# Attention with relative positions on one core: a narrower band product, moved behind the weighted sum, with its ends filled by GpSimd, and row maxima turned once a step

## The chip, the cores and the metric

The kernel runs on one core of a Trainium2 chip. The metric is the time of one execution on the device in microseconds (us). Its parts are TensorE (matmuls, PE, with its weight loads PEld), ScalarE (ACT), VectorE (DVE), GpSimd (POOL), SyncE (SP, which issues DMAs), the working memory SBUF and the matmul outputs' memory PSUM.

## What is computed

The reference is one transformer block: attention with 16 heads of 16 features on 8 sequences of 1024 tokens, a layer norm, a feed-forward layer with binarized weights and a second layer norm. The part that matters here is the attention with its relative bias:

```python
scores = jnp.einsum('bhid,bhjd->bhij', qh, kh)
rel = jnp.clip(pos[None, :] - pos[:, None], -K, K) + K
bias_r = jnp.einsum('bhid,rd->bhir', qh, rel_pe)
bias = jnp.take_along_axis(bias_r, jnp.broadcast_to(rel[None, None], (b, h, l, l)), axis=-1)
attn = jax.nn.softmax(scores + bias, axis=-1)
out = jnp.einsum('bhij,bhjd->bhid', attn, vh)
```

K is 64, so that a query has 129 different biases. Beyond a distance of 64 tokens the bias is that of an end of the table, and the kernel adds it to the keys beforehand. Only a band around the diagonal is left: for 128 queries, some 256 keys.

## The kernel before

Three stages follow each other: the projections (to about 250 us), the attention, and from about 2050 us the output projection with the feed-forward layer. The change touches the attention alone (lines 539 to 1138).

The attention goes over 64 steps, one for two heads of a sequence. The heads' rows lie in the upper and the lower half of the TensorE array, and their matmuls run side by side. Every engine has its own program for a step, and the order in each is written out by hand. A step on TensorE has eight pairs m of two units (pair, L1111), and it works on three things at once:

- Weighing, for this step's heads. A unit is one tile of 128 keys against half of the queries (512). turn_bands (L1041) transposes the parts of the band that lie in it into PSUM; only units near the diagonal have any. In pairs 0 and 4 each unit has two (over both heads), in the other pairs one unit has four and the other none, and the order of units (weighed, L638) puts the one with four first. weigh (L1059) adds the scores. ScalarE takes the exponential (expo, L899) into SBUF.
- The weighted sum of an earlier pair's exponentials with the values (weighted, L1077; lagging, L1091), eight matmul instructions.
- Looking, 24 units ahead: the scores are computed the other way round (look, L1022), and VectorE takes the maximum of each row with the band added (L933 to L963). GpSimd negates the maxima and splits them in a rounded part and a rest (minus_maxima, L807), TensorE transposes them (turn_max, L1033), ScalarE copies them out of PSUM (copy_turned, L894), and SyncE moves them into two extra rows of the queries (load_minus_max, L723), so that the scores come out of weigh with the maximum subtracted. This is done in two halves, at units 4 and 10 of a step (TURN_AT, L619).

The band product (band_product, L1008) for heads nearly three steps ahead multiplies 128 queries with the differences of the bias table. The table has 3 x 128 columns for each head: 128 differences, then 128 copies of the last one, then those for the last tile. The product has 256 columns. Every tile but the last uses the first two blocks, so that its columns 128 to 255 are all the same. ScalarE copies both heads' product to SBUF (copy_band, L886). For two tiles at a time SyncE writes them to memory (write_bands, L715), and GpSimd reads them back with rows one element shorter, which shifts each row against the one before and makes the band (read_bands, L784). GpSimd's own queue issues the loads of queries, keys and values too (step_of, L823).

Scores and band products use two PSUM buffers (weigh_ps) in turn. The order of use is first unit, band product, second unit, and then the same again with the buffers exchanged. So the band product waits for the exponential of the unit before the pair's first, the second unit for that of the first, and the next pair's first unit for the copy of the band (wait_for, L987). ScalarE's order is exponential, (in pair 1 the copy of the finished sums, L884), band copy, exponential. Each pair's order on TensorE is this:

```python
products(i, step, m, 0)
if bands_at(step, m):
    band_product(i, band_index(step, m))
lagging(i, step, m)
if step >= 0:
    turn_bands(i, step, m, 1)
products(i, step, m, 1)
```

## Time and profile before

| | |
|---|---|
| time, median of 3 runs | 2427.24 us (2426.69 to 2430.31) |
| the profiled execution, its own time | 2427.77 us |
| its span | 2426.1 us |
| TensorE busy | 2266.8 us (93%) |
| VectorE busy | 1742.5 us (72%) |
| ScalarE busy | 1669.9 us (69%) |
| GpSimd busy | 964.5 us (40%) |
| ScalarE, exponentials (L903) | 1048.8 us, 1024 of them |
| ScalarE, band copies (L891) | 302.8 us, 512 of them |
| TensorE, band products (L1017) | 202.4 us, 1024 of them |

Busy times overlap. A TensorE row's start is recorded and its end is modelled, and matmuls that are side by side or follow each other in the pipeline overlap in their durations. So the distance between two starts tells what work costs, and a row's duration tells when its result can be read. In a row of the timeline, x8 is the number of like instructions that it merges, and the brackets at its end give the idle time of the engine before it and who ended that.

### The profile page before, as it was taken

Reading aid. Unit: us, or ns where it says so; the run is one execution under the profiler, and the core shown is the slowest. Engines: PE = TensorE matmul, PEld = TensorE weight load, DVE = VectorE, ACT = ScalarE, POOL = GpSimd, SP = SyncE. Lnnn points to the kernel's source line nnn. Section 1 sums busy time; section 2 is a strip of 40 time slices with the busy share of each in tenths; the row PEclk is TensorE's granted clock in tenths of the full one; section 3 lists DMA queues with packets and bytes.
Section 4 is the critical chain, followed back from the end, with each engine's and each line's share of the span. In section 5 each row is a group of like instructions: output and inputs, shape, how many; then the busy total and the mean of one; then the engine's idle time right before and its main releaser. Section 6 shows DMA issues by size and latency. Waiting matters only on the chain. (4 is left out here: it accounts for less than half of the span.)

```text
span 2426.1 us, 47764 instructions
## 1 busy us (share of the span) xinstructions
PE 2266.8 (93%) x14642; PEld 1273.6 (52%) x14642; DVE 1742.5 (72%) x3444; ACT 1669.9 (69%) x2239; POOL 964.5 (40%) x1565
## 2 busy tenths in 40 slices
PE   4998599999999999999999999999999999799997
PEld 3555244444444444444444444444444444688886
DVE  2444467777777777777777777777777773588885
ACT  2443167777777777777777777777777777466766
POOL 0000444443444434443344433444334432466663
PEclk8999589999999999999999999999999999899999
DMA  6998777777777777777777777767767762333321
GB/s 179 357 335 317 216 186 204 204 209 207 204 207 200 208 207 204 203 205 205 204 204 204 209 207 202 204 201 208 210 199 207 201 196 88 104 99 108 108 63 44
DMA packets 335292, 468.58 MB, mean 193 GB/s; under 512 B 90517, under 2 KB 263270, under 8 KB 335206
## 3 DMA queue, kind: packets, MB, share of 16 engines
q0 software_dynamic: 120960, 215.78, 34.9%
q1 hardware_dynamic: 201206, 243.05, 30.1%
q10 hardware_dynamic: 13040, 8.80, 1.2%
q8 instruction: 30, 0.49, 0.1%
q14 instruction: 56, 0.46, 0.1%
HBM read 244.73 MB, written 221.25 MB: 192 GB/s over the span
## 5 line engine op out<-in xcount | busy, mean ns | idle before, releaser
L903 ACT ACTIVATE probs<-weigh_ps 128x1024 f32<-128x1024 f32 x1024 | 1048.8, 1025 | 403.7 <-PE weigh_ps L1069 400.4
L955 DVE CUSTOM_DVE_ANT_1 ring_ps<-ring_ps,band_all 128x512 f32<-128x512 f32 x1008 | 681.0, 715 | 265.9 <-PE ring_ps L1029 265.7
L1029 PE MATMUL ring_ps<-keys,queries 48*128 48x512 f32 x2048 | 839.2, 474 | 32.2 <-DVE partial_max L944 10.4
L1069 PE MATMUL weigh_ps<-queries,keys 50*128 50x512 f32 (+3 forms) x2688 | 752.7, 386 | 1.4 <-ACT probs L903 1.1
L944 DVE TENSOR_REDUCE partial_max<-ring_ps 128x2 f32<-128x1024 f32 x512 | 627.7, 1226 | 155.3 <-PE ring_ps L1029 115.0
L1029 PEld LDWEIGHTS ring_ps<-keys,queries 48*128 48x128 f32 x2048 | 370.6, 187 | 511.1 <-issue 394.5
L1086 PE MATMUL sum_ps<-probs,values 128*32 128x512 f32 x4096 | 547.3, 606 | 0.1
L1054 PE MATMUL weigh_ps<-ident,band_all 128*128 128x128 f32 x2048 | 362.7, 290 | 23.2 <-ACT carried L891 20.3
L1069 PEld LDWEIGHTS weigh_ps<-queries,keys 50*128 50x128 f32 x2688 | 356.7, 186 | 17.7 <-ACT probs L903 9.5
L790 POOL DMA_DIRECT2D band_all<-band_scr x320 | 230.6, 723 | 331.4 <-DMA band_scr<-carried 319.6
L1054 PEld LDWEIGHTS weigh_ps<-ident,band_all 128*128 128x128 f32 x2048 | 214.0, 141 | 246.2 <-ACT probs L903 104.6
L891 ACT ACTIVATE carried<-weigh_ps 128x512 f32<-128x512 f32 x512 | 302.8, 592 | 50.3 <-PE weigh_ps L1017 50.3
L1017 PE MATMUL weigh_ps<-rel_terms,queries 48*128 48x256 f32 x1024 | 202.4, 343 | 17.9 <-DMA queries<-q_scr 17.0
L1308 DVE TENSOR_TENSOR hidden<-gelu,hidden 128x512 fp32r<-128x512 f32 x128 | 146.3, 1160 | 46.3 <-ACT hidden L1409 45.2
L803 POOL DMA_DIRECT2D band_all<-band_scr x128 | 101.9, 796 | 187.7 <-DMA band_scr<-carried 165.2
L1478 PE MATMUL hid_ps<-x1T,sign1T 128*128 128x512 f32 x512 | 144.2, 404 | 12.9 <-ACT hidden L1409 11.6
L1407 ACT ACTIVATE gelu<-hid_ps,b_col,alpha 128x512 f32<-128x512 f32 x128 | 99.7, 779 | 77.4 <-PE hid_ps L1478 51.4
L1492 PE MATMUL out_ps<-sign2T,hidden 128*128 128x256 f32 x1024 | 150.4, 290 | 0.6 <-ACT hidden L1409 0.6
L955 DVE DVE_READ_ACCUMULATOR2_ANT partial_max<- 128x1 f32 x1024 | 145.1, 142 | 0.0
L1492 PEld LDWEIGHTS out_ps<-sign2T,hidden 128*128 128x128 f32 x1024 | 137.9, 188 | 9.5 <-ACT hidden L1409 0.8
L693 POOL DMA_DIRECT2D queries<-q_scr x128 | 80.6, 630 | 153.7 <-PE weigh_ps L1069 142.2
L1017 PEld LDWEIGHTS weigh_ps<-rel_terms,queries 48*128 48x128 f32 x1024 | 103.3, 189 | 55.1 <-ACT probs L903 30.9
(115 smaller groups left out, 1861.3 us busy)
## 6 DMA issues: line engine op xcount, KB each, us to landing
band_scr<-carried SPq DMA_DIRECT2D x256, 512.0 KB, 4.1
band_all<-band_scr POOLq DMA_DIRECT2D x128, 512.0 KB, 6.6
band_all<-band_scr POOLq DMA_DIRECT2D x128, 256.0 KB, 3.3
keys<-k_scr POOLq DMA_DIRECT2D x128, 240.0 KB, 9.0
k_scr<-k_parts SPq DMA_DIRECT2D x16, 1792.0 KB, 8.2
q_scr<-q_parts SPq DMA_DIRECT2D x16, 1024.0 KB, 6.2
queries<-q_scr POOLq DMA_DIRECT2D x128, 128.0 KB, 2.9
o_scr<-weighted_s SPq DMA_DIRECT2D x64, 256.0 KB, 9.1
```

What stands on the lines that cost most here:

```text
L790: pool.dma_start(band[:, c % SLOTS, m, :, e, c0:c1], flat(band_scr, band_base(c, m) + e * P * BAND_ROW + offset, [[BAND_ROW - 1, P], [2 * ...
L891: nc.scalar.activation(band_out[:, chunk % BANDS_OUT, :, e], weigh_ps[weigh_of["band", n]][:, :, 0:2 * P], ACT.Copy).then_inc(s_be, 1)
L903: nc.scalar.activation(probs[:, u % PROBS], weigh_ps[weigh_of["scores", at]][:], ACT.Exp).then_inc(s_pr, 1)
L944: nc.vector.reduce_max(partial_max[:, g, :, e, 0], ring_ps[:, first:second + 1], AX_X).then_inc(s_seen, HG)
L955: nc.vector.tensor_tensor_reduce(out=both, in0=both, in1=bias, scale=1.0, scalar=LOWEST, op0=ALU.add, op1=ALU.max, accum_out=partial_max[: ...
L1017: last = nc.tensor.matmul(dst[:, h, 0:2 * P].rearrange("p (a c) -> p a c", a=2), query_rows(c, h, ROWS, tile * P, (tile + 1) * P), moving, ...
L1029: nc.tensor.matmul(dst, query_rows(c, h, ROWS, tile * P, (tile + 1) * P), key_rows(c, h, ROWS, c0, c0 + 512), start=True, stop=True, tile_ ...
L1054: nc.tensor.matmul(weigh_ps[weigh_of["scores", at]][:, h, e * P:(e + 1) * P], band[:, c % SLOTS, tile // 2, h, tile % 2, side * P:(side + ...
L1069: last = nc.tensor.matmul(weigh_ps[weigh_of["scores", at]][:, h, e0 * P:e1 * P], key_rows(c, h, QROWS, k0, k0 + P), query_rows(c, h, QROWS ...
L1086: last = nc.tensor.matmul(sum_ps[r0:r0 + 32, :], values[:, c % SLOTS, v0:v0 + 32], probs[:, (2 * n + g) % PROBS, h], start=(n == 0), stop= ...
L1308: nc.vector.tensor_tensor(hidden[:, it % 2, 1, j], gelu[:, j % 2], hidden[:, it % 2, 0, j].bitcast(F32), ALU.subtract).then_inc(s_lo, 1)
L1492: last = nc.tensor.matmul(out_ps[:, t], hidden[:, it % 2, c, j, t * P:(t + 1) * P], sign2T[:, j], start=(c == 0 and j == 0), stop=(c == 1 ...
```

## The change

The band product of every tile but the last has 130 columns (NARROW), and ScalarE copies 130. GpSimd fills columns 130 to 255 from column 128 (fill_ends), for one or two tiles at a time, and SyncE's write waits for that. In TensorE's order the band product stands behind the weighted sum and the second unit's transposes, in front of the second unit's products; the order in which the PSUM buffers are used, and ScalarE's order, stay. The row maxima of both halves are negated, split, transposed, copied and moved together, at unit 10. Semaphores follow their new counts. The diff, cut to its core:

```diff
@@ -575,11 +576,11 @@
-row_max = sb("row_max", [P, 2, HG, QT], F32)
-negative = sb("negative", [P, 2, HG, QT], F32)
-negative_parts = sb("negative_parts", [P, 2, HG, PARTS, QT], F32)
-zero = sb("zero", [P, HG, QT], F32)
-minus_max = sb("minus_max", [HG * PARTS * QT, 2, P], F32R)
+row_max = sb("row_max", [P, HG, 2, QT], F32)
+negative = sb("negative", [P, HG, 2, QT], F32)
+negative_parts = sb("negative_parts", [P, HG, PARTS, 2, QT], F32)
+zero = sb("zero", [P, HG, 2, QT], F32)
+minus_max = sb("minus_max", [HG * PARTS * NT, P], F32R)
@@ -616,10 +618,10 @@
-TURN_AT = {4: 0, 10: 1}
+TURN_AT = 10
...
-    return u in TURN_AT and 0 <= step + 1 < G
+    return u == TURN_AT and 0 <= step + 1 < G
@@ -715,20 +717,20 @@
         c, m = n // NM, n % NM
-        sp.wait_ge(s_be, cnt(i, NT, 2 * n + 2))
+        sp.wait_ge(s_bf, cnt(i, NM, n + 1))
         sp.dma_start(flat(band_scr, band_base(c, m), [[BAND_ROW, P], [P * BAND_ROW, HG * 2], [1, 2 * P]]),
...
-    def load_minus_max(i, step, g):
+    def load_minus_max(i, step):
         c = step + 1
-        sp.wait_ge(s_tc, cnt(i, 2, 2 * c + g + 1))
+        sp.wait_ge(s_tc, cnt(i, 1, c + 1))
         for h in range(HG):
             r0 = h * ROW_TILE + ROWS
-            rows = queries[r0:r0 + PARTS, c % SLOTS, g * 512:(g + 1) * 512].bitcast(F32)
-            sp.dma_start(rows.rearrange("r (a p) -> r a p", a=QT),
-                         minus_max[h * PARTS * QT:(h + 1) * PARTS * QT, g, :].bitcast(F32)
-                         .rearrange("r (a p) -> r a p", a=1)).then_inc(s_min[g][c % SLOTS], 16)
+            rows = queries[r0:r0 + PARTS, c % SLOTS, :].bitcast(F32)
+            sp.dma_start(rows.rearrange("r (a p) -> r a p", a=NT),
+                         minus_max[h * PARTS * NT:(h + 1) * PARTS * NT, :].bitcast(F32)
+                         .rearrange("r (a p) -> r a p", a=1)).then_inc(s_min[c % SLOTS], 16)
@@ -804,16 +806,29 @@
-    def minus_maxima(i, step, g):
+    def minus_maxima(i, step):
         c = step + 1
-        done = cnt(i, 2, 2 * c + g + 1)
-        pool.wait_ge(s_rm, done)
-        nc.gpsimd.tensor_tensor(negative[:, g], zero[:], row_max[:, g], ALU.subtract)
-        nc.gpsimd.tensor_tensor(negative_parts[:, g, :, 0].bitcast(F32R), zero[:], row_max[:, g],
+        pool.wait_ge(s_rm, cnt(i, 2, 2 * c + 2))
+        nc.gpsimd.tensor_tensor(negative[:], zero[:], row_max[:], ALU.subtract)
+        nc.gpsimd.tensor_tensor(negative_parts[:, :, 0].bitcast(F32R), zero[:], row_max[:],
                                 ALU.subtract).then_inc(s_neg, 1)
-        pool.wait_ge(s_neg, done)
-        nc.gpsimd.tensor_tensor(negative_parts[:, g, :, 1], negative[:, g], negative_parts[:, g, :, 0],
+        pool.wait_ge(s_neg, cnt(i, 1, c + 1))
+        nc.gpsimd.tensor_tensor(negative_parts[:, :, 1], negative[:], negative_parts[:, :, 0],
                                 ALU.subtract).then_inc(s_mm, 1)
+
+    def fill_ends(i, step, quarter):
+        n = (step + BAND_STEPS) * NM + quarter - 2
+        if 0 <= n < G * NM:
+            pool.wait_ge(s_be, cnt(i, NT, 2 * n + 2))
+            pool.sem_inc(s_passed, 1)
+            tiles = 1 if n % NM == NM - 1 else 2
+            out = band_out[:, n % BANDS_OUT, :, 0:tiles]
+            last = None
+            for e in range(tiles):
+                end = out[:, :, e, P]
+                last = nc.gpsimd.tensor_copy(out[:, :, e, NARROW:2 * P],
+                                             flat(end, 0, [end.ap[0], end.ap[1], [0, P - 2]]))
+            last.then_inc(s_bf, 1)
@@ -825,23 +840,25 @@
             load_queries(pool, i, step + 3)
-        if 0 <= step + 1 < G:
-            minus_maxima(i, step, 0)
         read_chunk(i, step, 0)
+        fill_ends(i, step, 0)
         if 0 <= step and step + 3 < G:
...
             load_values(pool, i, step + 3)
+        fill_ends(i, step, 1)
         read_chunk(i, step, 1)
         if 0 <= step + 1 < G:
-            minus_maxima(i, step, 1)
+            minus_maxima(i, step)
         if step == -2:
             load_queries(pool, 0, 2)
+        fill_ends(i, step, 2)
         read_chunk(i, step, 2)
...
             load_values(pool, 0, 0)
+        fill_ends(i, step, 3)
         read_chunk(i, step, 3)
@@ -888,12 +905,13 @@
             act.wait_ge(s_bw[chunk % BANDS_OUT], cnt(i, 16 * NM // BANDS_OUT, 16 * (chunk // BANDS_OUT)))
-        nc.scalar.activation(band_out[:, chunk % BANDS_OUT, :, e], weigh_ps[weigh_of["band", n]][:, :, 0:2 * P],
-                             ACT.Copy).then_inc(s_be, 1)
+        width = 2 * P if n % NT == NT - 1 else NARROW
+        nc.scalar.activation(band_out[:, chunk % BANDS_OUT, :, e, 0:width],
+                             weigh_ps[weigh_of["band", n]][:, :, 0:width], ACT.Copy).then_inc(s_be, 1)
...
     def copy_turned(i, n):
-        act.wait_ge(s_turn, cnt(i, 2, n + 1))
-        nc.scalar.activation(minus_max[:, n % 2, :], ring_ps[0:HG * PARTS * QT, slot_of["turn", n], 0:P],
+        act.wait_ge(s_turn, cnt(i, 1, n + 1))
+        nc.scalar.activation(minus_max[:], ring_ps[0:HG * PARTS * NT, slot_of["turn", n], 0:P],
                              ACT.Copy).then_inc(s_tc, 1)
@@ -960,7 +978,7 @@
-        nc.vector.tensor_reduce(row_max[:, g], partial_max[:, g], AX_X, ALU.max).then_inc(s_rm, 1)
+        nc.vector.tensor_reduce(row_max[:, :, g], partial_max[:, g], AX_X, ALU.max).then_inc(s_rm, 1)
@@ -1012,10 +1030,12 @@
         for h in range(HG):
-            table = rel_terms[h * ROW_TILE:h * ROW_TILE + ROWS, :].rearrange("p (a c) -> p a c", a=3)
-            moving = table[:, 0:3:2] if tile == NT - 1 else table[:, 0:2]
-            last = nc.tensor.matmul(dst[:, h, 0:2 * P].rearrange("p (a c) -> p a c", a=2),
-                                    query_rows(c, h, ROWS, tile * P, (tile + 1) * P), moving,
+            table = rel_terms[h * ROW_TILE:h * ROW_TILE + ROWS, :]
+            product, moving = dst[:, h, 0:NARROW], table[:, 0:NARROW]
+            if tile == NT - 1:
+                product = dst[:, h, 0:2 * P].rearrange("p (a c) -> p a c", a=2)
+                moving = table.rearrange("p (a c) -> p a c", a=3)[:, 0:3:2]
+            last = nc.tensor.matmul(product, query_rows(c, h, ROWS, tile * P, (tile + 1) * P), moving,
                                     start=True, stop=True, tile_position=(h * ROW_TILE, 0))
@@ -1031,11 +1051,10 @@
-        g = n % 2
-        pe.wait_ge(s_mm, cnt(i, 2, n + 1))
+        pe.wait_ge(s_mm, cnt(i, 1, n + 1))
...
-        nc.tensor.transpose(dst[0:HG * PARTS * QT, 0:P],
-                            negative_parts[:, g].rearrange("p h c t -> p (h c t)"),
+        nc.tensor.transpose(dst[0:HG * PARTS * NT, 0:P],
+                            negative_parts[:].rearrange("p h c g t -> p (h c g t)"),
@@ -1043,7 +1062,7 @@
-            pe.wait_ge(s_min[g][c % SLOTS], i * (16 * HG) + 16 * HG * (c // SLOTS + 1))
+            pe.wait_ge(s_min[c % SLOTS], i * (16 * HG) + 16 * HG * (c // SLOTS + 1))
@@ -1114,11 +1133,11 @@
         products(i, step, m, 0)
-        if bands_at(step, m):
-            band_product(i, band_index(step, m))
         lagging(i, step, m)
...
             turn_bands(i, step, m, 1)
+        if bands_at(step, m):
+            band_product(i, band_index(step, m))
         products(i, step, m, 1)
...
     for step in range(-START, FIRST):
```

## Rows read from the trace of the kernel before

**Rows 1.** Windows: us, busy PE PEld DVE ACT POOL (instructions), clock, DMA share, GB/s.

```profile
1009.04:1036.45 27.41, 26.85 (x189) 13.38 (x189) 21.22 (x42) 21.06 (x28) 11.34 (x23) 1.00 0.72 205
1996.90:2023.40 26.50, 25.95 (x177) 12.43 (x174) 21.21 (x42) 18.28 (x22) 4.02 (x10) 1.00 0.27 87
```

**Rows 2.** Lines by form, 600 to 1800 us: xcount | busy us, mean ns.

```profile
L1069 PE MATMUL weigh_ps<-queries,keys 50*128 50x512 f32 x962 | 350.6, 446 | 0.0
...
L891 ACT ACTIVATE carried<-weigh_ps 128x512 f32<-128x512 f32 x350 | 207.2, 592 | 0.0
...
L1069 PE MATMUL weigh_ps<-queries,keys 50*128 50x128 f32 x262 | 66.6, 254 | 0.0
```

**Rows 3.** Waits, 600 to 1800 us: us in total, times, longest us.

```profile
PEld weigh_ps L1054 <- ACT probs L903: 73.8, 88, 0.9
...
PEld weigh_ps L1054 <- ACT carried L891: 55.7, 173, 0.6
```

**Rows 4.** Timeline of TensorE, pairs 2 to 7: start us, us, engine, line.

```profile
1009.04 1.07 PE L1086 MATMUL sum_ps<-probs,values 128*32 128x512 f32 x8
...
1015.48 1.07 PE L1086 MATMUL sum_ps<-probs,values 128*32 128x512 f32 x8
...
1019.38 1.06 PE L1086 MATMUL sum_ps<-probs,values 128*32 128x512 f32 x8
...
1025.88 1.07 PE L1086 MATMUL sum_ps<-probs,values 128*32 128x512 f32 x8
1026.90 0.50 PE L1029 MATMUL ring_ps<-keys,queries 48*128 48x512 f32 x1
...
1027.57 0.44 PE L1054 MATMUL weigh_ps<-ident,band_all 128*128 128x128 f32 x2
1027.94 0.49 PE L1029 MATMUL ring_ps<-keys,queries 48*128 48x512 f32 x1
...
1028.75 0.39 PE L1017 MATMUL weigh_ps<-rel_terms,queries 48*128 48x256 f32 x2
```

**Rows 5.** Timeline of TensorE, pair 0 to 1.

```profile
1029.06 1.06 PE L1086 MATMUL sum_ps<-probs,values 128*32 128x512 f32 x8
1030.06 0.44 PE L1054 MATMUL weigh_ps<-ident,band_all 128*128 128x128 f32 x2
...
1031.68 0.50 PE L1029 MATMUL ring_ps<-keys,queries 48*128 48x512 f32 x1
...
1032.59 1.06 PE L1086 MATMUL sum_ps<-probs,values 128*32 128x512 f32 x8
```

**Rows 6.** Timeline, pair 1 to 2.

```profile
1033.72 0.60 ACT L884 ACTIVATE weighted_s<-sum_ps 128x512 f32<-128x512 f32 x1 [0.25 <-PE sum_ps L1086]
...
1034.22 0.59 ACT L891 ACTIVATE carried<-weigh_ps 128x512 f32<-128x512 f32 x1
...
1034.86 0.66 PE L1054 MATMUL weigh_ps<-ident,band_all 128*128 128x128 f32 x4 [0.31 <-ACT carried L891]
...
1036.45 1.07 PE L1086 MATMUL sum_ps<-probs,values 128*32 128x512 f32 x8
```

**Rows 7.** Timeline, the stretch without band products.

```profile
2010.16 1.07 PE L1086 MATMUL sum_ps<-probs,values 128*32 128x512 f32 x8
2010.27 1.02 ACT L903 ACTIVATE probs<-weigh_ps 128x1024 f32<-128x1024 f32 x1 [0.51 <-PE weigh_ps L1069]
...
2011.34 0.50 PE L1029 MATMUL ring_ps<-keys,queries 48*128 48x512 f32 x1
...
2012.66 0.50 PE L1029 MATMUL ring_ps<-keys,queries 48*128 48x512 f32 x1
...
2013.34 1.07 PE L1086 MATMUL sum_ps<-probs,values 128*32 128x512 f32 x8
```

**Rows 8.** GpSimd: a wait in the timeline, a line's durations (ns min/median/max).

```profile
1016.81 0.20 POOL L811 TENSOR_TENSOR negative<-zero,row_max 128x8 f32<-128x8 f32 x1 [3.37 <-DVE row_max L963]
...
L873 POOL TENSOR_TENSOR carried<-band_all x2: 2367/2372/2376, 2048.8 to 2054.1; 128x1024 f32<-128x1024 f32 x2
```

More of the change, by code:

```diff
@@ L552, in post_ln_block @@
             BANDS_OUT = 4
+            NARROW = P + 2
             PROBS = 8
@@ L597, in post_ln_block @@
             s_be = sem("band_product_read")
+            s_bf = sem("band_ends_filled")
             s_bw = [sem(f"band_written{a}") for a in range(BANDS_OUT)]
@@ L607, in post_ln_block @@
             s_tc = sem("minus_max_copied")
-            s_min = [[sem(f"minus_max_in{g}_{a}") for a in range(SLOTS)] for g in range(2)]
+            s_min = [sem(f"minus_max_in{a}") for a in range(SLOTS)]
             s_sc = sem("scores_ready")
@@ L634, in turn_index @@
             def turn_index(step, u):
-                return 2 * (step + 1) + TURN_AT[u]
+                return step + 1
             def weighed(m):
@@ L740, in unit @@
                     if turns_at(step, u):
-                        load_minus_max(i, step, TURN_AT[u])
+                        load_minus_max(i, step)
                     if u == 5 and step > 0:
@@ L993, in wait_for @@
                         elif kind == "turn":
-                            pe.wait_ge(s_tc, cnt(i, 2, n + 1))
+                            pe.wait_ge(s_tc, cnt(i, 1, n + 1))
                         elif kind == "scores":
```

## The prediction

> **What bounds the kernel now.** I first read the stretches with their clock, then the lines by form, then who waited for whom, and last TensorE's starts within one step. One step of the loop takes 27.41 us at full granted clock; TensorE shows 26.85 us of it busy, ScalarE 21.06, VectorE 21.22, GpSimd 11.34 [rows 1]. Busy TensorE time is modelled at the ends, so I go by starts. A step has eight pairs. Each issues in order: first unit's transposes and products, band product, weighted sum, second unit's transposes and products. The starts of the weighted sums mark the pairs [rows 4 to 6].
>
> TensorE is almost a gapless chain, but it is laced to ScalarE through two PSUM buffers used in turn. In 1200 us (44 steps) weight loads of transposes stand 73.8 us behind exponentials and 55.7 us behind band copies [rows 3]. The stretch at the end with no band products says most: there a step still takes 26.50 us [rows 1], because the second unit's products must wait for the first unit's exponential. Weighted sum starts at 2010.16, exponential at 2010.27, products only at 2011.34 [rows 7]: 1.18 us, against 1.00 to 1.02 where TensorE sets the pace (1029.06 to 1030.06, 1025.88 to 1026.90 [rows 4, 5]). So a band product standing in front of the weighted sum hides little: taking it all away, copy and all, gives 0.9 us a step. What it costs where it stands is the question, and what the hole of 0.18 us behind the weighted sum can take in.
>
> **Part 1: 130 columns in place of 256** (seven tiles of eight). Matmuls of the same type take 254 ns at 128 columns and 446 at 512 [rows 2], 0.50 ns a column; there is no sign that short ones are streamed slower. 126 columns fewer are 0.06 us on each head's half of the array, and the heads run side by side: 0.06 us a product. ScalarE's copy takes 592 ns for 512 elements [rows 2] and 1.02 us for 1024 [rows 7], 0.84 ns an element on 0.16 fixed. For 260 elements that is 0.38 us, 0.21 us less. That is worth only what waits for the copy.
>
> **Part 2: the move.** First products to weighted sum is 0.91 us with a band product (1031.68 to 1032.59 [rows 5]) and 0.68 without (2012.66 to 2013.34 [rows 7]): it costs 0.23 where it stands, and with 130 columns about 0.18 in its new place. Only units near the diagonal have transposes. In six pairs (1, 2, 3, 5, 6, 7) the second unit has none, so the band product comes directly behind the weighted sum and fills the hole while the exponential ends: 1.00+0.18 = 1.18 us from weighted sum to second products, the same as the wait for the exponential. In pairs 0 and 4 there are two transposes, which wait for the exponential themselves, and the 0.18 come on top.
>
> Pair by pair, from one weighted sum to the next:
> - Pair 1 to 2, now 3.86 us (1032.59 to 1036.45). ScalarE does the copy of the weighted sum (from 1033.72), then the band copy (1034.22 to 1034.81), and the next transposes start at 1034.86 [rows 6]. New: the band copy ends 0.21 earlier; the transposes start 2.05 us after the weighted sum. From there it is now 1.59 us to the next one; without the band product, the turn and the second look's wait for its copy it is 0.59+0.68+0.07 = 1.34. Sum 3.39: -0.46 us.
> - Pair 7 to 0, now 3.18: 1.02, 0.67, 0.37, and 1.12 from products to weighted sum, where the band product waits for the exponential of the unit before [rows 4, 5]. New 1.18+0.67+0.37+0.70 = 2.92: -0.25.
> - Pairs 2, 3, 5, 6: together 16.84 us less pair 4's 3.90, so 12.94 [rows 4], 3.235 each. Without any band product such a pair takes 3.18 (2010.16 to 2013.34 [rows 7]). I take 3.20: -0.14 for the four.
> - Pair 0 to 1, now 3.53. New: 1.18, then 1.62 from transposes to the next products [rows 5] plus 0.18, then 0.68: 3.66, +0.13.
> - Pair 4 to 5, now 3.90 (1015.48 to 1019.38 [rows 4]): 0.18 for the exponential, 0.18 for the product, 0.23 less in front: +0.15 with the odd hundredths.
> Sum -0.57 us a step. Steps 0 to 60 of the 64 have both: 61 x 0.57 = 35 us.
>
> **Part 3: the ends by GpSimd.** Seven copies of 252 elements a step. GpSimd's shortest elementwise row is 0.20 us for 8 elements and the widest 2372 ns for 1024 [rows 8]; at the latter's rate 252 elements are 0.6 us. I take 0.5, bounds 0.2 and 2.4: 3.5 us a step (1.4 to 17) on an engine with 16 us free. The Trainium skill ("GPSIMD Engine Reference", section 3.1) gives 1.03 cycles an element for a body of one input; by that a copy would be some 0.2 us and a dispatch, a little under mine. The write to memory now waits for the fill, so it starts 0.5 to 1.0 us later, on SyncE's queue and in front of GpSimd's own reads. GpSimd waits for these reads anyway, and the bands are read a step and more before VectorE looks at them. Cost nothing, hidden by that lead. In GpSimd's queue the loads of keys and values stand behind the first fill, some 3 us later than now, for a head that is looked at a step later: nothing.
>
> **Part 4: maxima turned once.** Three small operations, one transpose, one copy of 0.25 us and two DMA issues less in a step; the half at pair 2 is counted above. The other waits for the row maxima as now: at 1016.81 GpSimd had idled 3.37 us for them [rows 8]. New in front of it are a wait for the band copy of pair 3, a fill of one tile and a read. The copy ends about 2.1 us after pair 3's weighted sum (1012.19), at 1014.3, the fill at 1014.8, the issue at 1015.8: 1.0 us before the maxima. Bound: nothing, or, if a fill takes 2.4 us, 1 us a step.
>
> The profiled execution took 2427.77 us (span 2426.1), the median of the runs is 2427.24. 2427.8-35 = 2393.
>
> **Rivals.** (a) *Small products are bound by their weight loads.* A load takes as long for 130 columns as for 256, so nothing would be saved by Part 1 on TensorE. The new slot is then 0.23 instead of 0.18: in pairs 0 and 4 in full, in the six others 0.05 beyond the hole. 8 x 0.05 x 61 = 24 us given back: 2417. For it: the heads' loads in front of every product. Against: the rows of 128 columns are the shortest. The Trainium skill ("TensorE: Matmul & The Clock Gate", section "Back-to-back issue gap") says that in a stream of loads and matmuls the spacing is set by both, 81 ns at 128 columns where columns alone give 56; by it a part of the saving fails. No row here separates them. 0.15.
> (b) *All of the exponential's wait goes.* If the pairs come down to the rate of the stretch without bands less the second turn, some 26.4 us a step, it is 61 us: 2367. 0.10.
> (c) *The wait for the band copy takes the place.* Slower. The copy now comes after the weighted sum, and the next pair's transposes need its PSUM buffer. Counted from the band product: 0.33 until it is done (0.39 [rows 4] less 0.06), the copy 0.38, and a signal each way, for which I take what an exponential's end needs to start TensorE (2011.29 to 2011.34 [rows 7]), 0.05: 0.81. TensorE is there at 0.18+0.67 = 0.85 [rows 4]. The slack is 0.04 us. Beyond it each 0.1 us in the copy or its signals is 0.6 us a step, so with 0.52 us for the copy the gain is gone, and at the old 0.59 the six pairs lose 0.17 each and pair 1 its 0.21: 1.23-0.57 = +0.66 us a step, 2468. Pair 3, which keeps 256 columns, pays it in any case. Against it stands only that ScalarE's time goes straight with the elements. 0.10. Two thirds of it (the copy at 0.52) cancel the gain: 2427, 0.09.
> (d) *GpSimd late with the maxima*, as under Part 4: TensorE waits at pair 5, up to 2454 (61 x 1.0 less 35). 0.03.
>
> **Numbers.** My forecast 0.53, (a) 0.15, (b) 0.10, cancelled 0.09, (c) 0.10, (d) 0.03. Faster by over 0.2% (about what a measurement of this kernel can tell from no change) 0.78, within it 0.09, slower 0.13. The forecast's own range is 2375 to 2412; with (a), (b) and the cancelled case it is 2370 to 2430, which leaves out (c), (d) and half of (b).
>
> **What would show it.** A step of 26.8 us; pair 1 to 2 at 3.4 and 7 to 0 at 2.9, pairs 0 and 4 longer than now by 0.1; ScalarE's band copy at 0.38; weight loads of transposes waiting less for exponentials; TensorE's look at its old duration. Wrong would be: transposes behind band copies at well over 56 us in the same stretch (c), the turn waiting for GpSimd over 0.4 us a step (d), 0.23 between band product and products (a), or fills over 1 us.

## The result, and the profile after

The changed kernel took 2482.98 us (median of four runs, 2480.8 to 2487.74) against 2428.58 us for the kernel before in the same comparison: ratio 1.0228, interval 1.0214 to 1.0242. It is slower by 2.3%, where 2393 us had been forecast, with a range of 2370 to 2430. In what follows, three executions that took far longer than the others of the same kernel (one of run 6, one of run 11, one of the kernel before in the comparison of runs 5 to 8) are left out of medians and ratios. The profiled execution took 2483.0 us, its span 2481.3.

The busy times of the page, after:

```profile
PE 2231.2 (90%) x14578; PEld 1195.0 (48%) x14578; DVE 1736.9 (70%) x3444; ACT 1619.9 (65%) x2175; POOL 1089.4 (44%) x1821
...
PEclk7999589999899999999999999999999999899999
```

Nothing became the bound by its work: TensorE and ScalarE are busy for less time than before, GpSimd for more but under half of the span. So the time is in waits, and in a lower TensorE clock (PEclk gives it in tenths of full speed; over the whole execution it averages 0.960, against 0.975 before). The next view shows where: three whole steps of the loop, in stretches as in [rows 1].

```profile
1087.92:1115.28 27.36, 26.13 (x190) 12.25 (x188) 21.19 (x44) 20.24 (x26) 13.41 (x27) 1.00 0.71 206
1144.50:1175.68 31.18, 28.72 (x189) 12.91 (x187) 21.13 (x42) 20.36 (x26) 13.34 (x27) 0.89 0.63 185
656.61:693.32 36.71, 33.15 (x189) 14.74 (x188) 21.30 (x44) 20.35 (x26) 13.32 (x27) 0.77 0.56 159
```

Two things are to be seen. The first step is undisturbed and takes 27.36 us, against 27.41 [rows 1]: the gain of 0.57 us a step did not come at all. The other two hold the same work and take 4 and 9 us longer, with the granted clock down to 0.89 and 0.77 of full speed. From the starts of the weighted sums, 31 of 60 steps are over 0.4 us longer than an undisturbed one. Together the 60 steps are 60 us longer than undisturbed ones; 41 of these lie in the 12 steps whose granted clock is below full, the rest in steps at full clock, of up to 29.2 us. Steps 0 to 60 of the loop take 1732.1 us where it took 1679.0: this is 53 of the 55 us between the two spans (2481.3 and 2426.1).

The waits of the same 1200 us (600 to 1800) as in [rows 3] name both troubles:

```profile
PEld weigh_ps L1038 <- ACT probs L921: 278.6, 253, 1.7
...
PEld weigh_ps L1073 <- ACT carried L909: 126.3, 295, 0.7
...
POOL band_all L805 <- DMA band_scr<-carried: 75.8, 36, 4.1
...
PEld ring_ps L1056 <- POOL negative_parts L816: 48.9, 42, 3.1
```

and the same view of the kernel before, of lines that did not stand ahead of the prediction:

```profile
PEld weigh_ps L1017 <- ACT probs L903: 22.1, 129, 0.2
...
PEld ring_ps L1037 <- POOL negative_parts L815: 16.6, 44, 0.5
```

The band product's weight loads (L1038) wait for the exponential 278.6 us where they waited 22.1. The turn of the maxima (L1056) waits for GpSimd 48.9 us where it waited 16.6, up to 3.1 us at a time, and GpSimd itself stands in front of a read (L805) for the write of a band. Idle time overlaps with work of other queues, so such sums are not the loss itself; they say where to look.

**The first trouble in a timeline.** Pair 2 of the undisturbed step, TensorE's products and ScalarE (start, us, engine, line; in brackets the idle time before and what ended it):

```profile
1087.92 1.07 PE L1105 MATMUL sum_ps<-probs,values 128*32 128x512 f32 x8
1088.02 1.02 ACT L921 ACTIVATE probs<-weigh_ps 128x1024 f32<-128x1024 f32 x1 [0.31 <-PE weigh_ps L1088]
...
1089.17 0.33 PE L1038 MATMUL weigh_ps<-rel_terms,queries 48*128 48x130 f32 x2 [0.19 <-ACT probs L921]
...
1089.33 0.44 PE L1049 MATMUL ring_ps<-keys,queries 48*128 48x512 f32 x1
...
1089.54 0.39 ACT L909 ACTIVATE carried<-weigh_ps 128x260 f32<-128x260 f32 x1 [0.49 <-PE weigh_ps L1038]
...
1089.98 0.66 PE L1073 MATMUL weigh_ps<-ident,band_all 128*128 128x128 f32 x4
...
1091.23 1.07 PE L1105 MATMUL sum_ps<-probs,values 128*32 128x512 f32 x8
```

The weighted sum ends at about 1088.99, but the band product starts only at 1089.17, when the exponential of 1088.02 is over. It does not lie beside the exponential; it stands behind it, and the products stand behind both. This pair has no transposes for its second unit. In the code, turn_bands for part 1 is called in every pair, and its wait_for of the "scores" buffer, which is the wait for that exponential, is executed whether or not a transpose follows. The band product is now the next instruction behind that wait.

**The second trouble.** GpSimd through the end of the step in front of the one at 1144.50 and on:

```profile
1143.31 0.74 POOL L829 COPY carried<-carried 128x252 f32<-128x252 f32 x2 [1.23 <-ACT carried L909]
1144.07 0.51 POOL L704 DMA_DIRECT2D keys<-k_scr  x1
...
1150.28 0.39 POOL L829 COPY carried<-carried 128x252 f32<-128x252 f32 x1 [2.65 <-ACT carried L909]
1153.46 0.78 POOL L805 DMA_DIRECT2D band_all<-band_scr  x1 [2.80 <-DMA band_scr<-carried]
1154.26 0.24 POOL L812 TENSOR_TENSOR negative<-zero,row_max 128x16 f32<-128x16 f32 x1
...
1154.74 0.22 POOL L816 TENSOR_TENSOR negative_parts<-negative,negative_parts 128x16 f32<-128x16 f32 x1
```

and the other engines' lines of the same stretch:

```profile
1144.08 0.36 SPq L721 DMA_DIRECT2D band_scr<-carried  x1
...
1152.56 0.16 DVE L981 TENSOR_REDUCE row_max<-partial_max 128x8 f32<-128x16 f32 x1
...
1155.02 0.28 PE L1056 MATMUL ring_ps<-ident,negative_parts 128*32 128x128 f32 x1 [1.41 <-POOL negative_parts L816]
...
1156.36 1.94 PE L1105 MATMUL sum_ps<-probs,values 128*32 128x512 f32 x8
```

VectorE has the row maxima at 1152.72. GpSimd is at that time held by the read of L805, which waits for the write that SyncE issued at 1144.08, behind the two fills. The read is issued from 1153.46, which takes 0.78 us, and the three small operations start 1.54 us after the maxima were there. TensorE's turn stands idle for them, and the next weighted sum takes 1.94 us in place of 1.07, at a granted clock of 0.51 (the last section has the row).

The transfers of the band to memory, from the view of DMA issues over the same 1200 us (count, size, median us from issue to landing), before:

```profile
band_scr<-carried SPq DMA_DIRECT2D x175, 512.0 KB, 3.9
```

and after:

```profile
band_scr<-carried SPq DMA_DIRECT2D x169, 512.0 KB, 5.7
```

Taken apart by pair in the trace, the write in question is issued 2.24 us after its pair's weighted sum before and 2.96 after, and lands 4.4 us later before (median; longest 6.7) and 7.9 us later after (longest 10.1), so 6.7 and 10.9 us after that weighted sum. The read is issued at 7.3 us before and at 11.5 after, and the row maxima come at 11.5 and 11.6. So the margin of some 3.5 us (11.5 less 7.3, less the 0.8 of issue) is used up in the median, and half of the steps are late.

### The profile page after: what moved, and what is told of

Same layout as the page of the kernel before. It is cut to its first block and busy times, and to the rows that moved or that the text cites. A ratio compares the mean times of both kernels' runs of the same rounds, so it can differ in the third digit from the quotient of the medians.

```text
span 2481.3 us, 47847 instructions
## 1 busy us (share of the span) xinstructions
PE 2231.2 (90%) x14578; PEld 1195.0 (48%) x14578; DVE 1736.9 (70%) x3444; ACT 1619.9 (65%) x2175; POOL 1089.4 (44%) x1821
## 5 line engine op out<-in xcount | busy, mean ns | idle before, releaser
L1049 PE MATMUL ring_ps<-keys,queries 48*128 48x512 f32 x2048 | 782.7, 453 | 20.0 <-DVE partial_max L962 10.2
L1088 PE MATMUL weigh_ps<-queries,keys 50*128 50x512 f32 (+3 forms) x2688 | 731.3, 380 | 1.4 <-ACT probs L921 0.8
L1105 PE MATMUL sum_ps<-probs,values 128*32 128x512 f32 x4096 | 560.0, 619 | 0.1
L829 POOL COPY carried<-carried 128x252 f32<-128x252 f32 x448 | 166.9, 400 | 723.7 <-ACT carried L909 720.6
L909 ACT ACTIVATE carried<-weigh_ps 128x260 f32<-128x260 f32 (+1 forms) x512 | 211.8, 414 | 327.3 <-PE weigh_ps L1038 327.3
L1049 PEld LDWEIGHTS ring_ps<-keys,queries 48*128 48x128 f32 x2048 | 355.5, 190 | 141.3 <-issue 79.9
L1088 PEld LDWEIGHTS weigh_ps<-queries,keys 50*128 50x128 f32 x2688 | 362.3, 189 | 12.2 <-ACT probs L921 9.5
L1038 PEld LDWEIGHTS weigh_ps<-rel_terms,queries 48*128 48x128 f32 x1024 | 102.8, 191 | 446.5 <-ACT probs L921 406.4
L1038 PE MATMUL weigh_ps<-rel_terms,queries 48*128 48x130 f32 (+1 forms) x1024 | 178.6, 339 | 80.3 <-ACT probs L921 61.6
L1327 DVE TENSOR_TENSOR hidden<-gelu,hidden 128x512 fp32r<-128x512 f32 x128 | 140.8, 1116 | 48.4 <-ACT hidden L1428 47.2
L805 POOL DMA_DIRECT2D band_all<-band_scr x128 | 101.5, 793 | 141.6 <-DMA band_scr<-carried 123.4
```

The lines of the kernel that those rows point to most:

```text
L909: nc.scalar.activation(band_out[:, chunk % BANDS_OUT, :, e, 0:width], weigh_ps[weigh_of["band", n]][:, :, 0:width], ACT.Copy).then_inc(s_b ...
L1038: last = nc.tensor.matmul(product, query_rows(c, h, ROWS, tile * P, (tile + 1) * P), moving, start=True, stop=True, tile_position=(h * ROW ...
L1049: nc.tensor.matmul(dst, query_rows(c, h, ROWS, tile * P, (tile + 1) * P), key_rows(c, h, ROWS, c0, c0 + 512), start=True, stop=True, tile_ ...
L1088: last = nc.tensor.matmul(weigh_ps[weigh_of["scores", at]][:, h, e0 * P:e1 * P], key_rows(c, h, QROWS, k0, k0 + P), query_rows(c, h, QROWS ...
L1105: last = nc.tensor.matmul(sum_ps[r0:r0 + 32, :], values[:, c % SLOTS, v0:v0 + 32], probs[:, (2 * n + g) % PROBS, h], start=(n == 0), stop= ...
```

## The experiments

The runs test two theories of the loss, each with the other as its rival, and what the three edits are worth. Step lengths are medians over steps 1 to 60 between weighted sums; "late" counts steps over 0.4 us longer than the tenth percentile. Each run is compared with the kernel before on the same chip (medians 2426.37 to 2429.39). Where a diff shows less than a run's text names, it is cut to the part that is new.

**1. The band product in front of the wait.**

```diff
                     lagging(i, step, m)
-                    if step >= 0:
-                        turn_bands(i, step, m, 1)
                     if bands_at(step, m):
                         band_product(i, band_index(step, m))
+                    if step >= 0:
+                        turn_bands(i, step, m, 1)
                     products(i, step, m, 1)
```

> The band product goes directly behind the weighted sum, in front of the second unit's wait and transposes; all else as in the changed kernel. Theory W (the second unit's wait for the exponential stands in the code in every pair, also where it has no transposes, and holds the product back): the undisturbed step falls from 27.37 to 26.7 to 26.9 us, weight loads of the product no longer wait for exponentials (278.6 us in 1200 before), the late steps at pair 4 to 5 stay: about 2450 us. Rival (the product is bound by its weight loads, its place is worth nothing): undisturbed step 27.3, about 2480.

2439.57 us, ratio 1.0041 (1.0013 to 1.0069), its runs from 2422.77 to 2451.0. The undisturbed step is 26.84 us, as expected; 28 of 60 steps are late, the longest pair 4 to 5 being 7.91 us, and the mean step is 27.71.

```profile
PEld weigh_ps L1038 <- ACT probs L921: 55.3, 59, 1.7
...
PEld ring_ps L1056 <- POOL negative_parts L816: 49.0, 43, 3.7
```

The product's wait falls from 278.6 to 55.3 us, the turn's stays at 49.0: the first trouble is this wait, and the second is another one. Removed alone, the wait is worth 43 us (2483.0 less 2439.6).

**2. The maxima in front of the read** that waits for the write.

```diff
                     fill_ends(i, step, 1)
-                    read_chunk(i, step, 1)
                     if 0 <= step + 1 < G:
                         minus_maxima(i, step)
+                    read_chunk(i, step, 1)
```

> GpSimd handles the row maxima before its second read of bands, product where the change put it. Theory M (the maxima are late because that read waits for a write that now starts later and lands after 3 to 9 us): pair 4 to 5 takes 4.0 us in every step, the turn's weight load waits for GpSimd under 10 us in 1200, every step 27.4: 2425 to 2430 us. Rival (the fills themselves, or their waits for the band copies, make GpSimd late): steps of 28 to 31 us stay, 2460 or more.

2419.28 us (2416.92 to 2421.48), ratio 0.9966 (0.9953 to 0.9979).

```profile
PEld weigh_ps L1038 <- ACT probs L921: 276.4, 263, 1.1
...
POOL negative L812 <- DVE row_max L981: 92.3, 43, 2.4
...
PEld ring_ps L1056 <- POOL negative_parts L816: 17.7, 43, 0.5
...
POOL band_all L805 <- DMA band_scr<-carried: 1.4, 2, 0.8
```

GpSimd waits for the maxima again and not the other way round, and one step of 60 is late. The write of pair 1 still lands 8.0 us after its issue, but nobody waits for it. The order of two entries in one queue is worth 64 us (2483.0 less 2419.3). The median step is now the undisturbed one, 27.37 us, and the product still waits 276.4 us: the first trouble alone keeps the kernel near its old time.

**3 and 11. Both edits**; run 11 is the same kernel again in a later comparison.

> Both edits. Theories W and M together: steps of 26.7 to 26.9 us throughout, 2390 to 2400 us. If only M holds: 2425 to 2430. If only W holds: about 2450.

> The kernel with both edits (product directly behind the weighted sum, maxima before the read) once more, beside the next one: 2384 to 2389 us.

2386.29 us (2385.21 to 2387.22), ratio 0.9824 (0.9807 to 0.9842), and again 2389.12, ratio 0.9843 (0.9829 to 0.9856). The step is as expected, the time a little under it. A step of it:

```profile
1124.79:1151.66 26.87, 26.64 (x190) 13.31 (x188) 21.21 (x42) 20.36 (x26) 13.35 (x27) 1.00 0.71 207
```

and its pair 7 to 0, which the forecast missed:

```profile
872.41 1.07 PE L1105 MATMUL sum_ps<-probs,values 128*32 128x512 f32 x8
872.52 1.02 ACT L921 ACTIVATE probs<-weigh_ps 128x1024 f32<-128x1024 f32 x1 [0.24 <-PE weigh_ps L1088]
873.41 0.33 PE L1038 MATMUL weigh_ps<-rel_terms,queries 48*128 48x130 f32 x2
873.67 0.49 PE L1049 MATMUL ring_ps<-keys,queries 48*128 48x512 f32 x1
...
873.78 0.39 ACT L909 ACTIVATE carried<-weigh_ps 128x260 f32<-128x260 f32 x1 [0.24 <-PE weigh_ps L1038]
...
874.47 0.43 PE L1073 MATMUL weigh_ps<-ident,band_all 128*128 128x128 f32 x2
874.83 0.50 PE L1049 MATMUL ring_ps<-keys,queries 48*128 48x512 f32 x1
...
875.59 0.64 PE L1105 MATMUL sum_ps<-probs,values 128*32 128x512 f32 x4
```

Here the product does start at the end of the weighted sum (873.41), as the forecast had it, and the exponential hides it but for 0.08 us: from the weighted sum to the products it takes 1.26 us where 1.18 were put. The pair takes 3.18 us and not 2.92. In this step the transposes come 0.80 us after the products and the weighted sum 1.12 us after the transposes; in the median of 45 steps it is 0.67, as forecast, and 1.25 where 0.37+0.70 were put. So 0.18 us are lost between the transposes and the weighted sum. In 34 of the 45 steps the second look product there waits for VectorE's reading of an earlier one; that this is the whole of the 0.18 is not shown.

**4. The product back at its old place**, with the narrow product, the fills, the single turn and the maxima in front of the read.

```diff
                     products(i, step, m, 0)
+                    if bands_at(step, m):
+                        band_product(i, band_index(step, m))
                     lagging(i, step, m)
                     if step >= 0:
                         turn_bands(i, step, m, 1)
-                    if bands_at(step, m):
-                        band_product(i, band_index(step, m))
```

> The band product back in front of the weighted sum, maxima before the read; narrow product, fills and single turn stay. If the place is worth nothing and the gain is the shorter copy and product and the single turn: steps of 26.7 to 26.9 us and within 10 us of the kernel with both edits, 2390 to 2405. If the forecast's reckoning of the place (0.05 us a pair and the released wait) holds: 15 to 25 us slower than the kernel with both edits.

2391.47 us, ratio 0.9844 (0.9826 to 0.9861); step 26.91. So even well placed behind the weighted sum, the move is worth 0.05 us a step, some 3 to 5 us, of the 35 to 40. The branch of the expectation by which the place is worth nothing holds. In the pairs the move gains in four and loses as much in two: 0 to 1 and 4 to 5 are shorter at the old place (3.47 and 3.85, against 3.55 and 4.04), 2 to 3 and 6 to 7 longer (3.35 and 3.30, against 3.17 twice).

**5. The move alone**, on the kernel before, with 256 columns and two turns (the diff is that of run 4 the other way round).

> The kernel before with nothing but the band product moved behind the second unit's transposes, at its old 256 columns, maxima in two halves, no fills. If the move is a loss that the narrow product hides: undisturbed step of 28.3 to 29.0 us, 2480 to 2520 us, transposes' weight loads waiting over 150 us in 1200 for band copies. If the forecast's reckoning of the place held (the product fills a hole in six pairs): at most +0.4 us a step, 2450 or less.

2522.35 us, ratio 1.038 (1.0359 to 1.0401); step 29.03, no late one.

```profile
PEld weigh_ps L1017 <- ACT probs L903: 253.8, 247, 1.1
...
PEld weigh_ps L1054 <- ACT carried L891: 168.6, 331, 0.7
```

The transposes wait 168.6 us for the wide copies, against 55.7 [rows 3], on top of the first trouble: behind the wait, the product breaks even only with the narrow copy and the single turn (27.36 us a step).

**6. The single turn alone**, on the kernel before (its product, place and writes unchanged; the read stands in front of the maxima).

```diff
-                    if 0 <= step + 1 < G:
-                        minus_maxima(i, step, 0)
                     read_chunk(i, step, 0)
...
                     read_chunk(i, step, 1)
                     if 0 <= step + 1 < G:
-                        minus_maxima(i, step, 1)
+                        minus_maxima(i, step)
```

> The kernel before with nothing but the maxima turned once, product of 256 columns in its old place, no fills, maxima still behind the second read in GpSimd's queue. If one turn less is worth what pair 1 to 2 saves: 0.15 to 0.25 us a step, 2411 to 2418 us. If the order of maxima and read is by itself enough to make the maxima late: late steps appear here too and the time is 2430 or more; if it takes the later write, the maxima still wait some 90 us or more in 1200 for the row maxima and no step is late.

2414.26 us, ratio 0.9939 (0.9916 to 0.9962); step 27.29, and one late step in 60. The order "read, then maxima" is harmless as long as the write lands in time: the loss needs the fills as well.

**7. The changed kernel without fills**: the write waits for the copies again, and the ends are set to zero once. The kernel so leaves out a part of the bias, and its results are wrong; it is for the time alone.

```diff
-                    sp.wait_ge(s_bf, cnt(i, NM, n + 1))
+                    sp.wait_ge(s_be, cnt(i, NT, 2 * n + 2))
...
-                    fill_ends(i, step, 0)
...
+                nc.gpsimd.memset(band_out[:, :, :, :, NARROW:2 * P], 0.0).then_inc(s_set, 1)
```

> The changed kernel without the fills: columns 130 to 255 of the bands are set to zero once and never filled, which leaves out that part of the bias; the write waits for ScalarE's copies as before. Undisturbed step unchanged, 27.3 to 27.4 us. If the fill's 0.4 to 0.8 us in front of the write is the larger part of the lateness: few late steps, 2425 to 2440 us. If the later band copy (the product's new place) is: most late steps stay, 2455 to 2480.

2425.8 us, ratio 0.9983 (0.9969 to 0.9996); two late steps, the step 27.37.

```profile
PEld ring_ps L1054 <- POOL negative_parts L816: 18.1, 44, 0.5
```

The lateness goes with the fills, 57 us of it (2483.0 less 2425.8), though the write still takes 5.7 us to land.

**8. Narrow product and fills alone**, at the old place and with two turns, on the kernel before.

```diff
-                    sp.wait_ge(s_be, cnt(i, NT, 2 * n + 2))
+                    sp.wait_ge(s_bf, cnt(i, NM, n + 1))
...
+                    width = 2 * P if n % NT == NT - 1 else NARROW
...
+                    fill_ends(i, step, 0)
```

> The kernel before with the product of 130 columns, copies of 130 and fills, product in its old place, maxima in two halves. If the gain of the kernel with both edits (40 us) is mostly the shorter copy and product: undisturbed step of 26.9 to 27.1 us and 2400 to 2410 us, with few late steps, since the band is copied early. If most of it is the place or the single turn: 2415 or more.

2423.05 us (2412.96 to 2432.86), ratio 0.9983 (0.9965 to 1.0001). This missed: some 2400 to 2410 had been expected. The undisturbed step is 27.02, 0.39 less than before and as expected, but 15 steps are late here too, where few had been expected.

```profile
PEld ring_ps L1060 <- POOL negative_parts L817: 30.7, 44, 2.3
```

With runs 1 to 7 this makes the pattern. Without fills (runs 5, 6, 7) none to two steps are late, at either place. With fills and the read in front of the last maxima it is 15 at the old place with two turns, and 28 (run 1) and 31 at the new one with one turn. With fills and the maxima in front (runs 2, 3, 4) it is one to three.

**9. The wait behind the look.** Run 3, and where the second unit has no transposes its wait stands behind the first look product.

```diff
-                    wait_for(i, weigh_before["scores", at])
+                    if part == 0 or any((n - t) % NT < 2 for t in range(g * QT, (g + 1) * QT)):
+                        wait_for(i, weigh_before["scores", at])
...
                     if step >= 0:
+                        if part == 1:
+                            wait_for(i, weigh_before["scores", position(step, m, 1)])
                         weigh(step, m, part, 1 - first)
```

> Both edits, and where the second unit has no transposes its wait for the exponential stands behind the first look in place of in front of it. If TensorE's own order still leaves a hole behind the product in pairs 2, 3, 6 and 7: up to 0.1 us each, 24 us or less, 2365 to 2380. If those pairs are set by the exponential of the first unit and the copy of the band: within 4 us of the kernel with both edits.

2378.53 us (2376.85 to 2382.71), ratio 0.9803 (0.9788 to 0.9818); step 26.70. That is 10.6 us less than run 11 in the same comparison. All of the gain is in pair 7 to 0, 3.18 to 3.03 us: the look does not need the exponential and goes out 0.10 us earlier. In pairs 2, 3 and 6 the next weighted sum comes no sooner for it.

**10. The loads of keys and values behind the maxima** in GpSimd's queue, on the changed kernel, to see whether they are what delays the write.

```diff
+                    fill_ends(i, step, 1)
+                    read_chunk(i, step, 1)
+                    if 0 <= step + 1 < G:
+                        minus_maxima(i, step)
                     if 0 <= step and step + 3 < G:
...
                         load_keys(pool, i, step + 3)
                         load_values(pool, i, step + 3)
-                    fill_ends(i, step, 1)
-                    read_chunk(i, step, 1)
-                    if 0 <= step + 1 < G:
-                        minus_maxima(i, step)
```

> The changed kernel with the loads of keys and values moved behind the maxima in GpSimd's queue; product, fills and the order of read and maxima as changed. If the write of pair 1's band lands late (median 7.9 us after its issue, 4.4 in the kernel before) because these loads start at the same moment: it lands after 3.3 to 5 us, hardly a step is late, 2422 to 2430 us. If the later start of the write (0.7 us) is enough by itself: it still lands in time only in part, late steps stay, 2445 or more.

2542.47 us, ratio 1.047 (1.0452 to 1.0487), 41 late steps. Neither expectation came: the write of pair 1 now took 6.3 us to land (median of 60), less than the 7.9 but not the 4.4 of before, and that of pair 5, beside which the loads now go out, took 9.4 us instead of 3.4. So a write took longer in this run when loads were issued beside it, but without them the write of pair 1 is still late: these loads are at most a part of its 7.9 us, and which transfers make up the rest stays open. The traces show two things that bear on it. The read of another band that is issued 2.8 us in front of the write takes longer as well, 8.9 us in the changed kernel where it took 5.8. And in run 6, where the write is issued at its old 2.24 us but other transfers have moved, it takes 5.2 us. So a later start of the write is not needed for a later landing.

**12. Two places.** Run 9, and in pairs 0 and 4, where the second unit has transposes, the product in front of the weighted sum again.

```diff
                     products(i, step, m, 0)
+                    if m % QT == 0 and bands_at(step, m):
+                        band_product(i, band_index(step, m))
                     lagging(i, step, m)
-                    if bands_at(step, m):
+                    if m % QT != 0 and bands_at(step, m):
                         band_product(i, band_index(step, m))
```

> The kernel whose wait stands behind the look, with the band product of pairs 0 and 4 (both units with transposes) back in front of the weighted sum and that of the other six behind it. The old place gave these two pairs 3.85 and 3.47 us to the next weighted sum against 4.04 and 3.55 in the new one, 0.27 less in sum, and will give back up to 0.2 in the pairs in front of them: a step of 26.5 to 26.7 us, 2366 to 2378. If the place of these two is worth nothing: within 3 us of 2378.5.

2365.39 us (2363.68 to 2367.76), ratio 0.9747 (0.9733 to 0.976), the fastest of all, and faster than both kernels. A step of it:

```profile
1138.90:1165.36 26.46, 26.21 (x189) 13.20 (x187) 21.22 (x42) 19.90 (x26) 13.43 (x27) 1.00 0.76 209
```

Pair 0 to 1 takes 3.29 us instead of 3.55 and pair 4 to 5 3.84 instead of 4.04. The pairs in front of them give back a part: 7 to 0 takes 3.21 instead of the 3.03 of run 9, and 3 to 4 takes 3.25 instead of 3.17.

## Why the prediction was wrong

Medians of the pairs over steps 1 to 60, us from one weighted sum to the next. "Forecast" is the prediction's; run 3 is the change with its two faults of order removed.

| pair | before | forecast | after | run 3 | run 4 | run 12 |
|---|---|---|---|---|---|---|
| 2 to 3 | 3.16 | 3.20 | 3.32 | 3.17 | 3.35 | 3.17 |
| 3 to 4 | 3.28 | 3.20 | 3.42 | 3.17 | 3.12 | 3.25 |
| 4 to 5 | 3.90 | 4.05 | 4.24 | 4.04 | 3.85 | 3.84 |
| 5 to 6 | 3.20 | 3.20 | 3.37 | 3.20 | 3.20 | 3.20 |
| 6 to 7 | 3.30 | 3.20 | 3.32 | 3.17 | 3.30 | 3.18 |
| 7 to 0 | 3.18 | 2.92 | 3.28 | 3.18 | 3.18 | 3.21 |
| 0 to 1 | 3.53 | 3.66 | 3.44 | 3.55 | 3.47 | 3.29 |
| 1 to 2 | 3.86 | 3.40 | 3.38 | 3.37 | 3.43 | 3.37 |

**Part 1 was right.** The copy of 260 elements takes 388 ns (0.38 forecast), and a fill 399, by the lines by form of the changed kernel:

```profile
L909 ACT ACTIVATE carried<-weigh_ps 128x260 f32<-128x260 f32 x295 | 114.5, 388 | 162.9 <-PE weigh_ps L1038 162.9
L829 POOL COPY carried<-carried 128x252 f32<-128x252 f32 x296 | 110.3, 399 | 487.7 <-ACT carried L909 484.9 <-DMA band_scr<-carried 2.8
```

The product's own saving can be read in the changed kernel, because pair 3 still has 256 columns at the same place:

```profile
1149.08 0.39 PE L1038 MATMUL weigh_ps<-rel_terms,queries 48*128 48x256 f32 x2 [0.19 <-ACT probs L921]
...
1149.29 0.39 PE L1049 MATMUL ring_ps<-keys,queries 48*128 48x512 f32 x1
```

From product to products there are 0.21 us here and 0.16 at 1089.17 with 130 columns; the medians are 0.22 (55 products) and 0.16 (272). In front of the weighted sum, the old place, it is 0.26 with 130 columns and 0.31 with 256 (medians of run 4). That is the forecast's 0.06 at either place.

**Part 2 failed at one sentence:** that in the six pairs without transposes for the second unit "the band product comes directly behind the weighted sum and fills the hole while the exponential ends". It reads the absence of transposes as the absence of turn_bands. The function waits first and then finds nothing to do, and in the kernel before that cost nothing, since the products behind it needed the same buffer. With the product behind it the wait costs nearly the whole gain: after, no pair but 0 to 1 and 1 to 2 is shorter than before, and the undisturbed step is 27.36. Run 2 against run 3, which differ in this order alone, puts it at 33 us (2419.3 less 2386.3). With both faults of order gone the kernel is 40 us faster than before (2426.4 less 2386.3), where 35 were forecast.

With the order as the sentence has it, the pair table holds: the step is 26.86 us where 26.84 comes out of the forecast. That it fits so closely is luck, since errors in it cancel. Pair 7 to 0 did not gain its 0.25 (3.18): its terms 1.18 and 0.37+0.70 were too small by 0.08 and 0.18. Against that, pair 0 to 1 took 3.55 and not 3.66, and pairs 2, 3 and 6 took 3.17. The credit was misplaced too. The text gave -0.39 of its -0.57 to pairs 7 and 2, 3, 5, 6, which is what the move was to bring; run 4 has 26.91 without any move. What pays is the narrow copy and product (step 27.02 in run 8, 0.39 less) and the single turn (27.29 in run 6, 0.12 less): the two add up to 26.90. The largest piece is pair 1 to 2, forecast at 3.40 and measured at 3.37 to 3.38.

**Parts 3 and 4 failed at the fills' consequence.** The fill was sized well, 0.37 to 0.40 us a copy against 0.5 taken, and so was the write's later start, 0.72 us (2.96 less 2.24) against 0.5 to 1.0. What failed is "Cost nothing, hidden by that lead". The lead of a step and more is that of the read's data. The read's issue is another thing: it holds GpSimd's queue until the write has landed, and Part 4 then counted in front of the maxima "a wait for the band copy of pair 3, a fill of one tile and a read" as copy, fill and issue, 1.0 us ahead of time. The wait for the write of pair 1's band to land, which the read carries, was left out, though Part 3 itself puts the write "in front of GpSimd's own reads". It stands there until 10.9 us after pair 1's weighted sum in the median, 4.2 us later than before: 0.72 for the start and 3.5 for the landing (7.9 less 4.4), which no term of the sum had. Run 2 takes it away by order alone and run 7 by taking the fills away: 64 and 57 us. With the 33 us of Part 2 this is the whole way from 2483 to 2386. The two are not independent: in the other order (run 1, then run 3) the wait counts 43 us and the maxima 53.

**The rivals.** (d) names the second cause in kind: GpSimd late with the maxima, TensorE waiting at pair 5. It was given 0.03 and a bound of one microsecond a step, since only a slow fill was thought to bring it; with single pairs of up to 7.19 us instead of 4.02, its bound was wrong as well. (c) did not decide: the transposes wait 126.3 us for copies, against 55.7 [rows 3], more than the prediction allowed itself, but run 3 still has 80.3 at 26.86 us a step. Run 5 bears out its direction: at 256 columns the moved product, behind its wait, costs 93 us (2522.35 less 2429.39). (a) is ruled out: it put 0.23 us between product and products, the rows above have 0.16, and 0.06 more with 256 columns. (The 0.26 at 873.41 is a wait for the exponential; with 256 columns it is 0.26 there too, in the median.) (b) did not come in any run of the change as made, though run 12, with further edits of order, reaches 2365, by 26.5 us a step.

## What to carry to other kernels

A semaphore wait is an instruction in its engine's order, also where the work that it guards is empty: before moving work past a function, read which waits the function executes, not which operations it issues. For small work on which others depend (here three operations of 0.2 us), list everything ahead of it in its queue and follow each wait back to the end, through a DMA to its landing with its longest duration and not only its median. And a part that costs nothing in a queue's own account may still start a transfer later, into the company of other transfers.

## What the hardware showed unexpectedly

- A write of 512 KB to memory whose issue moved by 0.72 us landed 7.9 us after its issue instead of 4.4 (medians of one write in four, among other transfers whose times had moved as well), and another went from 3.4 to 9.4 us when loads were issued beside it.
- Some short stalls of TensorE are followed by a lower clock, and two thirds of the delay lies in steps where that happens. In the changed kernel 12 of 60 steps have a granted clock below full, and they hold 41 of the 60 us of delay; the other late steps stay at full clock. Each of the twelve falls comes in a stall of TensorE of 1.1 to 2.6 us or up to 1.5 us behind its end; seven other stalls, of 1.0 to 1.8 us, are followed by none (all between 400 and 2000 us). In the step that began at 656.61 the granted clock averages 0.77 of full speed, so part of it ran at 1.2 GHz and the rest at 2.4, and the step takes 36.71 us for the work of 27.36. In the step from 1144.50 the engine stood idle for 1.41 us in front of 1155.02, then worked for 1.34 us at full clock, and then the clock fell:

```profile
1155.02:1156.36 1.34, 1.34 (x10) 0.80 (x10) 0.00 (x0) 0.27 (x1) 0.00 (x0) 1.00 0.99 256
1156.36:1158.39 2.03, 2.03 (x12) 0.37 (x11) 1.23 (x1) 1.02 (x1) 0.00 (x0) 0.51 0.39 145
```

  The eight matmuls of the weighted sum take 1.94 us instead of 1.07, and the slower pace outlasts the gap: the look products at 1158.49 and 1159.03 take 0.74 and 0.62 us, where at full clock they take 0.44 and 0.40. Idle time in many short pieces did not do this: in run 5 TensorE is busy for only 368 of 400 us (600 to 1000), and its granted clock there is 1.00.
